# Forming a group's messages before the next group's placing one-hot on VectorE, in a graph attention layer

## The chip, the cores and the metric

The kernel runs on one core of one Trainium2 chip. The metric is the device time of one execution in microseconds. Three runs of the kernel before gave 1275.45, 1272.54 and 1271.82 us, so its time is the median, 1272.54 us. The hardware profiler recorded one further execution, and all rows shown below come from it.

## The reference

There are 6250 nodes with 96 features and 100000 edges, sorted by the node that they point to. The reference computes, with 8 heads of 12 numbers:

```
Q, K, V = x@Wq+bq, x@Wk+bk, x@Wv+bv          # per node
E       = edge_attr@We + be                  # per edge
score   = exp(clip(sum_12(K[src] * Q[dst] / sqrt(12) * E), -5, 5))   # per edge and head
msg     = V[src] * score
wV, Z   = segment_sum(msg, dst), segment_sum(score, dst)             # per node
out     = layernorm(x + wV / (Z + 1e-6))
```

## The kernel before, in words

A first part, some 125 us long, computes the tables of K and V (`kv_table`) and of Q (`q_table`) for all nodes and writes them to HBM. Then the edges are worked through in 99 groups: 96 groups of 8 tiles of 128 edges, and three shorter ones. This edge pass is what the change touches. Its program is fully unrolled, and the order on every engine is the order in which the code is written; nothing is scheduled. Each engine waits on counting semaphores: `sum_done`, for example, is raised by one when a group's scatter matmuls are done.

For a group g the work goes through the engines like this.

- GpSimd (POOL) gathers K and V rows of the group's source nodes, one indirect DMA for each tile, 8 to a group (L377). They go into `kv`, a ring of 8 groups. So the gathers of group g wait until the messages of group g-8 are formed (`msg_done`, L363), since that is the last reading of that part of the ring. From group 48 on (`CLOSE`) they also wait until the query matmuls of group g-2 are done (`q_done`, L365).
- TensorE (PE) projects the edge attributes (`psE`, L434), picks the destination's query by a matmul with a one-hot (`psQ`, L440), transposes the product `qe` to edge rows (`psT`, L451), and adds the messages to the nodes by matmuls with another one-hot, `place` (`psA`, L496). In its order stand, for group g: transposes of g+1, `psE` and `psQ` of g+2, then the scatter into `psA` of g. The function is `products`.
- ScalarE (ACT) copies `psE` to `qe` (L601), and takes the exponential of the clipped scores into the last 8 columns of `msg` (L615). Before that exponential it waits until the scatter of group g-2 is done, since `msg` has two buffers (L614).
- VectorE (DVE) does, in the function `arithmetic`: `qke` = transposed scores times K (L866), `qe` of the next group (L786), the sums over 12 (`logit`, L875), the clip (`clipped`, L881), the one-hot `place` of group g+1 (`make_place`, L774, which waits until the scatter of group g-1 is done, because `place` has two buffers), the messages `msg` of g (L890) and the one-hot `pick` of group g+3 (`make_pick`, L765).
- SyncE (SP) issues the other loads: the query windows `qwin`, two groups of edge attributes at a time (768 KB) and every fourth group a block of `rel_table` (1008 KB). They are issued as `q_done` rises.

Every four groups a block of nodes is finished. After the last scatter of a block, ACT copies `psA` out (L609), PE turns it (L461), and VectorE normalises it in twelve steps, `block_step` 0 to 11, strewn over the next groups. `between(n)` issues the step that stands for place n of the group by the table `BLOCK_PLACES`: in a block's first group, step 0 (`rzb`, L800) stands between `logit` and the clip, step 1 (L802) after the clip, step 2 (`yb`, L804) between `place` and `msg`, step 3 (L810) after `msg`. PE may begin the next block's scatter only when step 2 is done. In the third group, step 9 (L828) stands before `place`, step 10 (L831) between `place` and `msg`, and step 11 (`ob`, L838) after `msg`.

## Time and profile before

| | before |
|---|---|
| median of three runs | 1272.54 us |
| profiled execution: first to last instruction | 1265.2 us |
| what the runs have around that, against the median | 7.3 us |
| PE busy | 694.1 us (55%) |
| DVE busy | 620.3 us (49%) |
| ACT busy | 180.9 us (14%) |
| POOL busy | 758.5 us (60%) |
| granted TensorE clock, mean | 0.723 of full speed |

No engine is busy for more than 60% of the span. A busy share is an average over stages with different limits, so what the kernel is worth waiting for must be read from the waits. In the waits "remote" means that the profile found no instruction that ended just when the wait ended.

### The profile page before, as it was taken

Reading aid. Unit: us, or ns where it says so; the run is one execution under the profiler, and the core shown is the slowest. Engines: PE = TensorE matmul, PEld = TensorE weight load, DVE = VectorE, ACT = ScalarE, POOL = GpSimd, SP = SyncE. Lnnn points to the kernel's source line nnn. Section 1 sums busy time; section 2 is a strip of 40 time slices with the busy share of each in tenths; the row PEclk is TensorE's granted clock in tenths of the full one; section 3 lists DMA queues with packets and bytes.
Section 4 is the critical chain, followed back from the end, with each engine's and each line's share of the span. In section 5 each row is a group of like instructions: output and inputs, shape, how many; then the busy total and the mean of one; then the engine's idle time right before and its main releaser. Section 6 shows DMA issues by size and latency. Waiting matters only on the chain.

```text
span 1265.2 us, 11863 instructions
## 1 busy us (share of the span) xinstructions
PE 694.1 (55%) x3376; PEld 477.0 (38%) x3376; DVE 620.3 (49%) x1205; ACT 180.9 (14%) x343; POOL 758.5 (60%) x788
## 2 busy tenths in 40 slices
PE   4655646454445446436585575575545555565554
PEld 4554333243234324324353333343324333343332
DVE  1221435454355346436594554554545544544556
ACT  1224201111011011101120110110111110110111
POOL 7371456666656656656536566666666666666660
PEclk8657767768667767767796776677676786687777
DMA  7464254354355345444455445445435454454440
GB/s 185 156 198 139 79 149 128 102 158 130 105 142 139 106 127 150 115 125 127 135 144 146 125 114 157 127 115 156 126 105 164 129 140 133 127 135 135 121 115 28
DMA packets 89940, 165.51 MB, mean 131 GB/s; under 512 B 43315, under 2 KB 61908, under 8 KB 86840
## 3 DMA queue, kind: packets, MB, share of 16 engines
q1 hardware_dynamic: 52843, 89.34, 25.6%
q0 software_dynamic: 37024, 75.35, 21.4%
q8 instruction: 28, 0.46, 0.2%
q14 instruction: 45, 0.37, 0.1%
HBM read 152.22 MB, written 12.39 MB: 130 GB/s over the span
## 4 chain that ended last, share of the span: by engine, by line
another core or an unknown queue 40%; PE 21%; issue 17%; DVE 13%; ACT 6%; DMA 2%; SPq 0%; DVEq 0%
PE psE L434 7%; DVE qe L786 5%; ACT qe L601 5%; PE psA L496 4%; PE psT L451 4%; DVE logit L875 2%; DMA xt<-xT 1%; DVE msg L890 1%; PE psQ L416 1%; DVE qke L866 1%; PE psA L461 1%; PE psE L404 1%; DVE clipped L881 1%; DVE ob L838 1%
## 5 line engine op out<-in xcount | busy, mean ns | idle before, releaser
L377 POOL DMA_INDIRECT kv<-kv_table,idx x750 | 726.7, 969 | 468.7 <-issue 221.4
L496 PE MATMUL psA<-place,msg 128*104 128x104 f32 x1564 | 210.4, 301 | 289.9 <-DVE msg L890 220.6
L496 PEld LDWEIGHTS psA<-place,msg 128*104 128x104 f32 x1564 | 198.5, 213 | 318.6 <-DVE msg L890 235.0
L434 PE MATMUL psE<-ea,we 97*96 97x512 f32 x392 | 256.3, 790 | 0.0
L774 DVE TENSOR_TENSOR place<-psI,rel_tile 128x832 f32<-128x832 f32 (+1 forms) x99 | 98.5, 995 | 293.9 <-remote 293.9
L451 PE MATMUL psT<-identity,qe 96*128 96x96 f32 x782 | 114.7, 307 | 153.0 <-DVE qe L786 124.0
L601 ACT ACTIVATE qe<-psE 96x1024 f32<-96x1024 f32 (+1 forms) x99 | 99.9, 1009 | 622.0 <-remote 469.4
L786 DVE TENSOR_TENSOR qe<-psQ,qe 96x1024 f32<-96x1024 f32 (+1 forms) x99 | 119.1, 1203 | 82.3 <-ACT qe L601 33.8
L451 PEld LDWEIGHTS psT<-identity,qe 96*128 96x128 f32 x782 | 96.9, 181 | 165.1 <-DVE qe L786 128.3
L866 DVE TENSOR_TENSOR qke<-psT,kv 128x768 f32<-128x768 f32 (+1 forms) x99 | 92.9, 938 | 87.6 <-remote 86.9
L434 PEld LDWEIGHTS psE<-ea,we 97*96 97x96 f32 x392 | 75.8, 218 | 79.3 <-issue 79.3
L890 DVE TENSOR_TENSOR msg<-kv,msg 128x768 f32<-128x768 f32 (+1 forms) x99 | 93.0, 940 | 0.2
L875 DVE TENSOR_REDUCE logit<-qke 128x64 f32<-128x768 f32 (+1 forms) x99 | 91.5, 924 | 0.0
L440 PE MATMUL psQ<-q_parts,qwin 126*96 126x512 bf16 x196 | 69.7, 441 | 0.0
L615 ACT ACTIVATE msg<-clipped 128x64 f32<-128x64 f32 (+1 forms) x99 | 25.3, 256 | 259.2 <-DVE clipped L881 155.0
L440 PEld LDWEIGHTS psQ<-q_parts,qwin 126*96 126x96 bf16 x196 | 29.5, 150 | 79.9 <-issue 79.9
L765 DVE TENSOR_SCALAR q_parts<-q_parts,query_id 126x1024 bf16<-126x1024 bf16 x99 | 47.5, 481 | 12.2 <-DMA q_parts<-rel_table 12.2
L461 PE MATMUL psA<-identity,accT 104*128 104x104 f32 x73 | 17.3, 362 | 57.6 <-ACT accT L609 29.0
L800 DVE TENSOR_SCALAR rzb<-psA 128x24 f32<-128x24 f32 (+1 forms) x25 | 4.5, 181 | 68.2 <-PE psA L461 43.0
L375 POOL DMA_INDIRECT xg<-xrows,idx x32 | 31.3, 978 | 11.1 <-issue 9.5
L461 PEld LDWEIGHTS psA<-identity,accT 104*128 104x128 f32 x73 | 11.0, 208 | 62.6 <-ACT accT L609 32.8
L404 PE MATMUL psE<-wn,xt 97*128 97x192 f32 x52 | 16.3, 467 | 18.7 <-issue 14.6
(107 smaller groups left out, 356.8 us busy)
## 6 DMA issues: line engine op xcount, KB each, us to landing
ea<-eaT SPq DMA_DIRECT2D x49, 768.0 KB
q_parts<-rel_table SPq DMA_DIRECT2D x24, 1008.0 KB
kv<-kv_table,idx POOLq DMA_INDIRECT x750
qwin<-q_table SPq DMA_DIRECT2D x198, 23.6 KB
xb<-xrows SPq DMA_DIRECT2D x24, 144.0 KB
out<-ob SPq DMA_DIRECT2D x24, 144.0 KB
q_table<-q_parts SPq DMA_DIRECT2D x4, 720.0 KB
kv_table<-kv SPq DMA_DIRECT2D x2, 960.0 KB
```

Of the source, the lines that this page charges most:

```text
L377: pool.indirect_dma_start(kv[:, k, t], None, kv_table, sources).then_inc(kv_in[k], 16)
L434: last = nc.tensor.matmul(psE[0:D, h, 0:size], we[:], ea[:, k // 2 % 2, edge:edge + size], start=True, stop=True)
L440: last = nc.tensor.matmul(psQ[0:D, h, 0:size], qwin[0:QR, k % QRING, h], pick[0:QR, k % 2, h * GE // 2:h * GE // 2 + size], start=True, st ...
L451: last = nc.tensor.transpose(psT[:, t % 2, t // 2 * D:(t // 2 + 1) * D], qe[0:D, k % 2, t * P:(t + 1) * P], identity[0:D, 0:D])
L496: last = nc.tensor.matmul(psA[0:ML, off:off + PW], msg[:, s, t], place[:, s, t], start=opens, stop=closes)
L601: nc.scalar.activation(qe[0:D, k % 2, 0:edges], psE[0:D].rearrange("d b e -> d (b e)")[:, 0:edges], ACT.Copy).then_inc(e_up, 1)
L765: nc.vector.tensor_scalar(pick[0:QR, k % 2], rel[0:QR, k // BG % 2, k % BG * GE:(k % BG + 1) * GE], query_id[0:QR], None, ALU.is_equal).th ...
L774: nc.vector.tensor_tensor(place[:, k % 2, 0:nt], ps_ids[:, 0:PW].unsqueeze(1).broadcast_to([P, nt, PW]), rel_tile[:, bass.ds(g * T, nt)].u ...
L786: nc.vector.tensor_tensor(qe[0:D, k % 2, 0:edges], psQ[0:D].rearrange("d b e -> d (b e)")[:, 0:edges], qe[0:D, k % 2, 0:edges], ALU.mult). ...
L866: nc.vector.tensor_tensor(qke[:, 0:nt].rearrange("p (t b) d -> p b t d", **by_bank), psT[:, :, 0:nt // 2 * D].rearrange("p b (t d) -> p b ...
L875: nc.vector.tensor_reduce(logit[:, 0:nt * H], qke[:, 0:nt].rearrange("p t (h d) -> p (t h) d", h=H), AX.X, ALU.add).then_inc(logit_done, 1)
L890: nc.vector.tensor_tensor(msg[:, s, 0:nt, 0:D].rearrange("p t (h d) -> p t h d", h=H), kv[:, k, 0:nt, D:2 * D].rearrange("p t (h d) -> p t ...
```

## The change

On VectorE, `make_place` of the next group is moved from before the messages to behind them. The block steps of places 2 and 3 then stand directly behind each other, ahead of `msg`; the step of place 4 stands between `msg` and `place`. The wait of VectorE on `sum_done` ahead of `msg` is dropped; the wait on `wt_done`, which ScalarE raises only after its own wait on the same count of `sum_done`, stays. Nothing else is changed: the other engines have the same instructions in the same order.

```diff
                         nc.vector.tensor_scalar(clipped[:, s, 0:nt * H], logit[:, 0:nt * H], -5.0, 5.0, ALU.max,
                                                 ALU.min).then_inc(clip_done, 1)
                         between(2)
-                        if at + 1 < NG:
-                            make_place(r, k + 1, at + 1)
                         between(3)
-                        if at >= 2:
-                            dve.wait_ge(sum_done, g - 1)
                         dve.wait_ge(wt_done, g + 1)
                         nc.vector.tensor_tensor(
                             msg[:, s, 0:nt, 0:D].rearrange("p t (h d) -> p t h d", h=H),
                             kv[:, k, 0:nt, D:2 * D].rearrange("p t (h d) -> p t h d", h=H),
                             msg[:, s, 0:nt, D:ML].unsqueeze(3).broadcast_to([P, nt, H, HD]), ALU.mult).then_inc(msg_done, 1)
                         between(4)
+                        if at + 1 < NG:
+                            make_place(r, k + 1, at + 1)
                         if at + 3 < NG:
                             make_pick(r, k + 3, at + 3)
                         between(5)
```

VectorE in the first two groups of a block, before (`rzb`, `yb`, `bn`, `stat` belong to the block that has just ended; `q_parts` is the place in memory where `pick` lies):

```order
L881 TENSOR_SCALAR clipped<-logit 128x64 [waits logit_done,wt_done]
L802 RECIPROCAL rzb<-rzb 128x24 [waits block_steps]
L774 TENSOR_TENSOR place<-psI,rel_tile 128x832 [waits sum_done]
L804 TENSOR_TENSOR yb<-psA,rzb 128x288 [waits block_steps]
L890 TENSOR_TENSOR msg<-kv,msg 128x8x96 [waits wt_done,sum_done]
L810 TENSOR_TENSOR yb<-yb,xb 128x288 [waits xb_in1,block_steps]
L765 TENSOR_SCALAR q_parts<-q_parts,query_id 126x1024 [waits q_done,rel_in0]
L813 BN_STATS bn<-yb 128x6 [waits block_steps]
L813 BN_STATS bn<-yb 128x6 x2
L866 TENSOR_TENSOR qke<-psT,kv 128x2x4x96 [waits kv_in1,t_done]
```

The same place after the change (the message line is L886 there):

```order
L881 TENSOR_SCALAR clipped<-logit 128x64 [waits logit_done,wt_done]
L802 RECIPROCAL rzb<-rzb 128x24 [waits block_steps]
L804 TENSOR_TENSOR yb<-psA,rzb 128x288 [waits block_steps]
L886 TENSOR_TENSOR msg<-kv,msg 128x8x96 [waits wt_done]
L810 TENSOR_TENSOR yb<-yb,xb 128x288 [waits xb_in1,block_steps]
L774 TENSOR_TENSOR place<-psI,rel_tile 128x832 [waits sum_done]
L765 TENSOR_SCALAR q_parts<-q_parts,query_id 126x1024 [waits q_done,rel_in0]
L813 BN_STATS bn<-yb 128x6 [waits block_steps]
L813 BN_STATS bn<-yb 128x6 x2
L866 TENSOR_TENSOR qke<-psT,kv 128x2x4x96 [waits kv_in1,t_done]
```

`place` has moved two places back, behind the messages and step 3, and takes its wait on `sum_done` with it.

VectorE in the third group of a block, before:

```order
L881 TENSOR_SCALAR clipped<-logit 128x64 [waits logit_done,wt_done]
L828 TENSOR_SCALAR spread<-spread 128x3 [waits block_steps]
L774 TENSOR_TENSOR place<-psI,rel_tile 128x832 [waits sum_done]
L831 TENSOR_TENSOR spread<-spread 128x3 [waits block_steps]
L890 TENSOR_TENSOR msg<-kv,msg 128x8x96 [waits wt_done,sum_done]
L838 TENSOR_SCALAR ob<-yb,stat,spread 128x96 [waits block_steps,ob_out]
L838 TENSOR_SCALAR ob<-yb,stat,spread 128x96 x2
L765 TENSOR_SCALAR q_parts<-q_parts,query_id 126x1024 [waits q_done,rel_in1]
```

And after the change:

```order
L881 TENSOR_SCALAR clipped<-logit 128x64 [waits logit_done,wt_done]
L828 TENSOR_SCALAR spread<-spread 128x3 [waits block_steps]
L831 TENSOR_TENSOR spread<-spread 128x3 [waits block_steps]
L886 TENSOR_TENSOR msg<-kv,msg 128x8x96 [waits wt_done]
L838 TENSOR_SCALAR ob<-yb,stat,spread 128x96 [waits block_steps,ob_out]
L838 TENSOR_SCALAR ob<-yb,stat,spread 128x96 x2
L774 TENSOR_TENSOR place<-psI,rel_tile 128x832 [waits sum_done]
L765 TENSOR_SCALAR q_parts<-q_parts,query_id 126x1024 [waits q_done,rel_in1]
```

Here the three instructions that write the finished rows come between the messages and `place` too.

## Rows read from the trace of the kernel before

**Rows 1.** The page, part 4: shares of the chain that ended last.

```profile
another core or an unknown queue 40%; PE 21%; issue 17%; DVE 13%; ACT 6%; DMA 2%; SPq 0%; DVEq 0%
```

**Rows 2.** Waits from 165.3 to 594.5 us: who waited for what, us, times, longest.

```profile
DVE place L774 <- remote: 181.1, 16, 13.1
POOL kv L377 <- issue: 80.1, 263, 0.3
POOL kv L377 <- DVE msg L890: 79.2, 17, 5.9
DVE rzb L800 <- PE psA L461: 23.8, 9, 12.4
```

**Rows 3.** Timeline, 600 to 624 us: start, us, engine, line [idle before, its end].

```profile
600.91 0.94 DVE L866 TENSOR_TENSOR qke<-psT,kv 128x768 f32<-128x768 f32 x1
...
603.76 1.88 PE L434 MATMUL psE<-ea,we 97*96 97x512 f32 x4
603.95 0.19 DVE L881 TENSOR_SCALAR clipped<-logit 128x64 f32<-128x64 f32 x1
604.18 0.26 ACT L615 ACTIVATE msg<-clipped 128x64 f32<-128x64 f32 x1 [2.90 <-issue]
...
613.49 0.95 POOL L377 DMA_INDIRECT kv<-kv_table,idx  x1 [0.31 <-issue]
617.25 1.02 DVE L774 TENSOR_TENSOR place<-psI,rel_tile 128x832 f32<-128x832 f32 x1 [13.10 <-remote]
617.40 1.02 ACT L601 ACTIVATE qe<-psE 96x1024 f32<-96x1024 f32 x1 [12.96 <-remote]
618.19 0.95 DVE L890 TENSOR_TENSOR msg<-kv,msg 128x768 f32<-128x768 f32 x1
619.05 0.48 DVE L765 TENSOR_SCALAR q_parts<-q_parts,query_id 126x1024 bf16<-126x1024 bf16 x1
619.19 3.10 PE L496 MATMUL psA<-place,msg 128*104 128x104 f32 x16 [13.12 <-DVE msg L890]
619.41 0.95 POOL L377 DMA_INDIRECT kv<-kv_table,idx  x1 [4.97 <-DVE msg L890]
619.45 0.95 DVE L866 TENSOR_TENSOR qke<-psT,kv 128x768 f32<-128x768 f32 x1
620.32 1.21 DVE L786 TENSOR_TENSOR qe<-psQ,qe 96x1024 f32<-96x1024 f32 x1
```

**Rows 4.** Windows: us, busy of PE, PEld, DVE, ACT, POOL (instructions), clock, DMA, GB/s.

```profile
604.70:617.20 12.50, 1.37 (x5) 0.33 (x3) 0.00 (x0) 0.00 (x0) 7.56 (x8) 0.75 0.32 89
625.00:651.00 26.00, 22.90 (x132) 13.81 (x132) 24.80 (x49) 6.09 (x12) 3.79 (x4) 0.94 0.48 132
```

**Rows 5.** Groups of instructions on POOL, 165.3 to 594.5 us: busy, mean ns, idle.

```profile
L377 POOL DMA_INDIRECT kv<-kv_table,idx x280 | 271.8, 971 | 159.3 <-issue 80.1 <-DVE msg L890 79.2
```

**Rows 6.** The same on POOL, 675.5 to 1195.5 us.

```profile
L377 POOL DMA_INDIRECT kv<-kv_table,idx x352 | 339.8, 965 | 179.4 <-issue 108.0 <-remote 70.5 <-PE psQ L440 0.9
```

**Rows 7.** Timeline, 699 to 724 us: a cycle behind group 48.

```profile
699.71 0.95 POOL L377 DMA_INDIRECT kv<-kv_table,idx  x1 [3.33 <-remote]
...
706.78 1.63 PE L496 MATMUL psA<-place,msg 128*104 128x104 f32 x16
...
716.64 1.02 DVE L774 TENSOR_TENSOR place<-psI,rel_tile 128x832 f32<-128x832 f32 x1 [6.61 <-remote]
...
722.32 0.96 DVE L866 TENSOR_TENSOR qke<-psT,kv 128x768 f32<-128x768 f32 x1 [2.60 <-remote]
722.38 1.02 ACT L601 ACTIVATE qe<-psE 96x1024 f32<-96x1024 f32 x1 [12.13 <-remote]
723.44 0.94 POOL L377 DMA_INDIRECT kv<-kv_table,idx  x1 [4.02 <-issue]
```

**Rows 8.** Timeline, 599 us: a gather beside the messages.

```profile
598.93 0.95 DVE L890 TENSOR_TENSOR msg<-kv,msg 128x768 f32<-128x768 f32 x1
...
599.60 1.10 POOL L377 DMA_INDIRECT kv<-kv_table,idx  x1 [0.30 <-issue]
```

## The prediction, as it was made before the changed kernel was run

> **What bounds the kernel now.** I read the page first and found no busy engine; the largest share of the chain that ended last, 40%, is idle time that ends with a semaphore whose giver the profile can't name [rows 1]. So I read the waits of a steady stretch next. From 165.3 to 594.5 us VectorE stands 181.1 us before `place`, in 16 waits of up to 13.1 us, all "remote", and POOL stands 79.2 us before a gather until VectorE has formed messages, in 17 waits [rows 2]. `place` waits for one thing alone, the scatter of the group before the last. The timeline shows what is odd about it. PE ends `psE` at 603.76 + 1.88 = 605.6 us; ACT, which waits for just that, begins at 617.40, after 12.96 us of idling, and VectorE's `place` at 617.25 after 13.10 us [rows 3]. In that time PE, DVE and ACT do next to nothing while POOL issues its 8 gathers [rows 4]. What PE has finished is seen by the others only after POOL has stopped: the last gather ends at 613.49 + 0.95 = 614.4, the wait ends 2.8 us later. I call this a hold. A second place shows its beginning: the gathers start at 699.71, the scatter ends at 706.78 + 1.63 = 708.4, 8.7 us into them, and `place`, which waits for it, starts at 716.64 [rows 7]. What VectorE and ACT give to each other is not held: at 603.95 and 604.18 the exponential follows the clip at once, while PE's results are already late [rows 3].
>
> So the pass up to group 48 goes in cycles. POOL gathers as long as messages have been formed 8 groups back, PE's results come through in roughly the first 7 to 9 us, then all stand until POOL itself runs out of messages and stops. Between 165.3 and 594.5 us there are 280 gathers, 35 groups; 429.2 / 35 = 12.26 us for a group. Of that POOL's own pace is (271.8 + 80.1) / 280 = 1.257 us for a gather, 10.05 us for a group, and the 79.2 us of waits make 2.26 [rows 5, 2]. A typical cycle is 16 gathers and a pause of 4.97 us: 2.8 us until the hold ends, and then 617.25 to 619.41, 2.2 us, in which VectorE does `place` and `msg` [rows 3]. Without gathers the same work runs free: 5 messages in 26.0 us with VectorE busy for 24.8 of them [rows 4], some 6 us a group.
>
> **The change part by part.** It removes no instruction and adds none; a wait on `sum_done` goes that ACT has already made, worth 0.
>
> *Messages during the hold.* In the cycle shown, the exponential ends at 604.18 + 0.26 = 604.4. With `place` no longer ahead, the messages are formed at about 604.5 to 605.4, instead of 618.19 to 619.14. POOL needs them at 614.4, so this pause of 4.97 us goes. That is the gain one sees first. But what is late next is the following group's messages, and for these VectorE needs `psT` from PE, which is held until POOL stops. So the pause isn't removed, it comes one group later.
>
> *The pause in the steady state.* When the hold ends, VectorE now stands before `place` with the messages already spent. Ahead of the next `msg` are then `place` 0.94 (start to start, 617.25 to 618.19), `pick` 0.40 (619.05 to 619.45), `qke` 0.87 (to 620.32), `qe` 1.21, `logit` about 0.9, the clip 0.3, the exponential 0.3, and `msg` 0.95 with 0.3 to POOL's start [rows 3]: 6.1 us instead of 2.2. If instead the query or edge result of the next group was caught by the hold, VectorE stands before `qe`: 1.2 for ACT's copy, then 1.2 + 0.9 + 0.3 + 0.3 + 0.95 + 0.3 = 5.1. Where it is a block's first group, VectorE stands before `rzb`, which needs the last scatter copied and turned; after that only clip, exponential, step 2 and `msg` are left, about 3.8. The mean is 5.0, and the whole pause 2.8 + 5.0 = 7.8 us in place of 5.0.
>
> *How many groups fit a cycle.* The clock of the hold starts with POOL. With the messages of two groups formed by some 13 us after the hold's end, the third needs PE's `psE` and `psQ` of a further group; going through the durations of [rows 3] I find these finished about 8 to 9 us after POOL has started again, just where the hold sets in (8.7 us was too late in [rows 7]). So I take two groups in most cycles and three in one of four. With two, a cycle is 2 x 10.05 + 7.8 = 27.9 us, 13.95 a group, 1.7 more than now. With three, (30.15 + 7.8) / 3 = 12.65, 0.4 more. A block's first group can't be formed in a hold at all, since `rzb` waits on the last scatter; that cuts cycles of three short. A quarter of the cycles with three gives about 1.35 a group, for 35 groups +47 us. At the end of the stretch POOL must wait anyhow until PE has caught up, and one pause less is in the way: -5.
>
> *Behind group 48.* There POOL waits for `q_done` and not for messages: 70.5 us remote and 0.9 us by name on 44 groups [rows 6]. At a hold's end VectorE stands before `qke` [rows 7], and after the change it will stand there as well; `qe`, PE and the next gather follow it as before. Here I take 0. Bounds: the message comes 0.94 earlier where `place` isn't held (below nothing: -0.9 for each of 25 cycles, -22), or a `pick` that is made later costs a query result, one extra pause of 4.0 in a few cycles, +20.
>
> *The gap that `place` filled.* Between clip and `msg` lies the exponential, 0.3 us with its semaphores; `place` stood there. Now VectorE idles for it where no block step stands at place 2. That costs only where VectorE sets the pace, the 26 us of [rows 4] and a little more: 7 groups by 0.3, +2. If it were on the path everywhere it would be 99 x 0.3 = 30.
>
> *Gathers beside messages.* The gather that starts at 599.60 beside `msg` takes 1.10 us, the others 0.95 [rows 8, 3]. That is 0.15 by 35, at most +5, and mostly the same pairs meet already; I take 0. The Trainium skill (GPSIMD Engine Reference, Specifications) says that VectorE instructions with two SBUF inputs contend with GpSimd for its SBUF interface, which speaks against forming messages during gathers; by a full lock of 0.95 us for each message it would be +33, by the row at most +5, and the row decides.
>
> The sum against the profiled execution: 1265.2 + 47 - 5 + 0 + 2 = 1309; with the 7.3 us by which the median stands above its span, 1317 us, 3.5% slower.
>
> **The rivals.**
>
> *Nearly all cycles hold three groups.* For it: the results of PE are only about a microsecond late. Against it: the block's first group. 35 x 0.4 - 5 + 2 = +11, 1284 us. If on the contrary all hold two, it is 35 x 1.7 - 3 = +56, 1329 us.
>
> *Faster: the hold opens while POOL runs on.* In [rows 7] `place` got its semaphore at 716.64, in the midst of the gathers and not after them; there loads of SP were in flight. If with messages formed ahead POOL runs on over such openings, the pause stays 5 us but comes once in three groups or more: (30.15 + 5.0) / 3 = 11.7, 0.55 less than now, 35 x 0.55 = 19 us; with no pauses at all it would be all 79 us of [rows 2]. I take -32 for it, 1240 us. It decides from the point at which a cycle holds four groups at my pause, or three with the old one. Against it: in the stretch of [rows 2] 16 waits make 181 us, so most last to POOL's stop.
>
> *No effect.* POOL's pauses only shift and the sum of a cycle stays: one group more before each pause, a longer pause behind it. That is between the two above, 1272 us.
>
> **How the numbers follow.** Mostly two groups a cycle (the forecast, and all two): 0.50. Nearly all three: 0.17. No effect: 0.11. Faster: 0.18. Something worse behind group 48 on top: 0.04. A difference of 0.3%, 4 us, is what a measurement of this kernel can tell from none. That gives slower 0.70, same 0.12, faster 0.18. The range goes from 1248, which takes in most of the faster case, to 1342, the all-two case with 13 us of the bound behind group 48. The forecast's own range is 1295 to 1335.
>
> **What would show it.** Right: up to group 48 POOL's waits for messages are fewer than 17 but their sum grows from 79 to about 125 us; VectorE's waits before `place` shrink while those before `qe` (for ACT's copy or the query result), `rzb` and `qke` grow; messages lie in the midst of gathers where nothing else moves; POOL's pace stays at 1.26 us. Behind group 48 the cycle stays at 23 to 24 us for 16 gathers. Wrong: runs of 24 or 32 gathers with pauses of 5 us, then it is faster; or 16 gathers with the pauses of now. If VectorE's busy time or POOL's mean of 971 ns changes by more than 3%, something is at work that I haven't seen.

## The result, and the profile after

| | before | changed |
|---|---|---|
| median of 4 runs each, same chip | 1273.99 us (1271.82 to 1277.34) | 1317.16 us (1304.74 to 1323.02) |
| ratio | | 1.031, 95% interval 1.026 to 1.036 |
| span of the profiled execution | 1265.2 us | 1321.3 us (its own time 1323.02) |

The changed kernel is 3.1% slower, 1317.16 us where 1317 was forecast. That is better than the forecast deserves: one of its terms was 15 us too large and two were 5 and 10 us too small. And on another chip, on which nothing of what is called a hold occurs, the same change made the kernel 1.5% faster. Both are shown below.

The page of the changed kernel, its span, busy times and the chain that ended last:

```profile
span 1321.3 us, 11766 instructions
PE 701.4 (53%) x3376; PEld 470.2 (36%) x3376; DVE 638.9 (48%) x1205; ACT 180.4 (14%) x343; POOL 758.5 (57%) x788
another core or an unknown queue 41%; PE 21%; issue 18%; DVE 13%; ACT 5%; DMA 1%; SPq 0%; DVEq 0%
```

The shares of the chain are those of before within a point [rows 1], and POOL is busy for exactly as long, 758.5 us. So the loss isn't work. It is in the waits. First POOL's, in the stretch of the changed kernel that answers to [rows 2] (188.3 to 620.6 us, 33 groups in 13 unbroken runs of gathers), then the group of its gathers, which answers to [rows 5]:

```profile
POOL kv L377 <- DVE msg L886: 102.3, 13, 10.1
```

```profile
L377 POOL DMA_INDIRECT kv<-kv_table,idx x264 | 255.2, 967 | 179.6 <-DVE msg L886 102.3 <-issue 77.3
```

A wait for messages is now 102.3 / 13 = 7.9 us long, against 79.2 / 17 = 4.7 before [rows 2], and there are 13 of them for 33 groups instead of 17 for 35. A gather's own pace is (255.2 + 77.3) / 264 = 1.259 us, as before.

What VectorE waits for in the same stretch, changed kernel:

```profile
DVE qke L866 <- remote: 57.7, 15, 6.8
DVE qe L786 <- remote: 43.3, 8, 8.2
DVE place L774 <- remote: 41.6, 8, 13.8
DVE place L774 <- PE psA L496: 32.4, 3, 15.8
DVE qe L786 <- ACT qe L601: 23.4, 14, 7.2
DVE rzb L800 <- PE psA L461: 9.3, 6, 5.3
```

And the kernel before, from 165.3 to 594.5 us, beside the rows for `place` and `rzb` in [rows 2]:

```profile
DVE qe L786 <- remote: 3.8, 2, 1.9
DVE qe L786 <- ACT qe L601: 3.4, 4, 1.1
DVE qke L866 <- remote: 1.0, 2, 0.6
```

The waits before `place` fall from 181.1 us to 41.6 + 32.4 = 74.0, those before `qe` and `qke` rise from some 8 us to 124. VectorE now meets the hold at whatever it does next with something from PE.

One whole cycle of the changed kernel, three groups long, from its timeline (start, us, engine, line [idle before, what ended it]). POOL has been gathering since 399.61:

```profile
405.47 1.88 PE L434 MATMUL psE<-ea,we 97*96 97x512 f32 x4
...
407.19 0.60 PE L440 MATMUL psQ<-q_parts,qwin 126*96 126x512 bf16 x2
...
412.38 0.96 DVE L866 TENSOR_TENSOR qke<-psT,kv 128x768 f32<-128x768 f32 x1 [3.06 <-remote]
414.52 1.02 ACT L601 ACTIVATE qe<-psE 96x1024 f32<-96x1024 f32 x1 [8.66 <-remote]
416.65 1.22 DVE L786 TENSOR_TENSOR qe<-psQ,qe 96x1024 f32<-96x1024 f32 x1 [3.31 <-remote]
...
419.55 0.96 DVE L886 TENSOR_TENSOR msg<-kv,msg 128x768 f32<-128x768 f32 x1 [0.32 <-ACT msg L615]
420.78 0.94 POOL L377 DMA_INDIRECT kv<-kv_table,idx  x1 [1.11 <-issue]
...
425.06 0.33 PE L496 MATMUL psA<-place,msg 128*104 128x104 f32 x1 [0.98 <-issue]
...
429.53 0.95 POOL L377 DMA_INDIRECT kv<-kv_table,idx  x1 [0.30 <-issue]
...
433.54 1.02 DVE L774 TENSOR_TENSOR place<-psI,rel_tile 128x832 f32<-128x832 f32 x1 [13.03 <-remote]
433.69 1.02 ACT L601 ACTIVATE qe<-psE 96x1024 f32<-96x1024 f32 x1 [14.18 <-remote]
434.88 0.95 DVE L866 TENSOR_TENSOR qke<-psT,kv 128x768 f32<-128x768 f32 x1
435.74 1.21 DVE L786 TENSOR_TENSOR qe<-psQ,qe 96x1024 f32<-96x1024 f32 x1
...
438.51 0.96 DVE L886 TENSOR_TENSOR msg<-kv,msg 128x768 f32<-128x768 f32 x1
439.74 0.94 POOL L377 DMA_INDIRECT kv<-kv_table,idx  x1 [9.26 <-DVE msg L886]
```

Read it from the end. The last gather ends at 429.53 + 0.95 = 430.48, the hold 3.0 us later (`place` and ACT's copy start together, 433.54 and 433.69). Then VectorE goes through `place`, `pick`, `qke`, `qe`, `logit`, the clip and `msg` before POOL may go on at 439.74: 6.2 us, and 9.26 in all, where the kernel before had 2.8 + 2.2 [rows 3]. The upper lines show why three groups fit: PE's results do reach the others in the midst of the gathers, one by one, 7 to 9 us late. `psE` ends at 405.47 + 1.88 = 407.35 and ScalarE copies it at 414.52; `psQ` ends at 407.79 and `qe` starts at 416.65. And the third group's messages at 419.55 come just in time (POOL stands for 1.11 us instead of 0.30). Between 423 and 433 us PE itself does nine of the sixteen scatter matmuls of a group in pieces, one every 0.7 to 2.1 us; the last seven follow in a row from 433.46, as the hold ends.

Behind group 48, the gathers that answer to [rows 6] (719.1 to 1249.3 us), and POOL's waits there:

```profile
POOL kv L377 <- remote: 59.8, 18, 4.1
POOL kv L377 <- PE psQ L440: 21.4, 6, 10.2
```

The 352 gathers take 530.2 us instead of 520.0. The wait for query results by name grew from 0.9 to 21.4 us. Nearly all of that are two pauses, 10.18 us before the gather at 890.63 and 9.98 us before that at 1037.2, each behind 24 gathers in a row. The first of them:

```profile
883.83 0.49 ACT L609 ACTIVATE accT<-psA 104x384 f32<-104x384 f32 x1 [15.90 <-remote]
...
886.24 3.20 PE L434 MATMUL psE<-ea,we 97*96 97x512 f32 x4
...
888.30 0.48 DVE L765 TENSOR_SCALAR q_parts<-q_parts,query_id 126x1024 bf16<-126x1024 bf16 x1
...
889.27 0.60 PE L440 MATMUL psQ<-q_parts,qwin 126*96 126x512 bf16 x2
...
890.63 0.94 POOL L377 DMA_INDIRECT kv<-kv_table,idx  x1 [10.18 <-PE psQ L440]
```

Here the hold caught the last scatter of a block: ScalarE could copy `psA` only at 883.83, after 15.90 us of idling. `psQ` begins as `psE`, which stands ahead of it on PE, comes to its end (886.24 + 3.20 = 889.44); `pick` was ready before that, at 888.78. The second pause has the same form.

Where the spans differ, 1321.3 - 1265.2 = 56.1 us: the time to the first gather of the edge pass proper 148.5 - 140.6 = 7.9, in the first part, which the change doesn't touch and where one load landed later (VectorE waited 30.7 us for it, before 14.8); from there to the first gather of group 48, 549.2 - 511.4 = 37.8; behind it 623.6 - 613.2 = 10.4. The profiled execution is also the slowest of its four, which lie between 1304.74 and 1323.02 us, so a term of 5 or 10 us, read from one execution of each kernel, is of the size of what executions differ by.

### The profile page after: what moved, and what is told of

Its sections match the earlier page's. It is cut to its first block, busy times and chain, and to the rows that moved or that the text cites. A ratio compares the mean times of both kernels' runs of the same rounds, so it can differ in the third digit from the quotient of the medians.

```text
span 1321.3 us, 11766 instructions
## 1 busy us (share of the span) xinstructions
PE 701.4 (53%) x3376; PEld 470.2 (36%) x3376; DVE 638.9 (48%) x1205; ACT 180.4 (14%) x343; POOL 758.5 (57%) x788
## 3 DMA queue, kind: packets, MB, share of 16 engines
q1 hardware_dynamic: 52843, 89.34, 24.3%
## 4 chain that ended last, share of the span: by engine, by line
another core or an unknown queue 41%; PE 21%; issue 18%; DVE 13%; ACT 5%; DMA 1%; SPq 0%; DVEq 0%
PE psE L434 8%; DVE qe L786 5%; PE psT L451 4%; ACT qe L601 4%; DVE logit L875 2%; PE psA L496 2%; DVE qke L866 1%; PE psQ L416 1%; DMA xt<-ones 1%; DVE msg L886 1%; DVE q_parts L765 1%; DVE place L774 1%; PE psE L404 1%; DVE clipped L881 1%
## 5 line engine op out<-in xcount | busy, mean ns | idle before, releaser
L434 PE MATMUL psE<-ea,we 97*96 97x512 f32 x392 | 274.6, 840 | 0.0
L451 PE MATMUL psT<-identity,qe 96*128 96x96 f32 x782 | 120.1, 317 | 278.0 <-DVE qe L786 195.5
L496 PE MATMUL psA<-place,msg 128*104 128x104 f32 x1564 | 195.7, 271 | 93.8 <-issue 92.3
L496 PEld LDWEIGHTS psA<-place,msg 128*104 128x104 f32 x1564 | 182.0, 186 | 116.8 <-issue 105.0
L434 PEld LDWEIGHTS psE<-ea,we 97*96 97x96 f32 x392 | 79.8, 229 | 84.9 <-issue 84.9
L886 DVE TENSOR_TENSOR msg<-kv,msg 128x768 f32<-128x768 f32 (+1 forms) x99 | 93.6, 946 | 17.5 <-ACT msg L615 10.9
L461 PEld LDWEIGHTS psA<-identity,accT 104*128 104x128 f32 x73 | 10.9, 208 | 178.6 <-ACT accT L609 159.9
L440 PE MATMUL psQ<-q_parts,qwin 126*96 126x512 bf16 x196 | 72.8, 459 | 0.0
```

Source lines behind the costliest of these rows:

```text
L434: last = nc.tensor.matmul(psE[0:D, h, 0:size], we[:], ea[:, k // 2 % 2, edge:edge + size], start=True, stop=True)
L440: last = nc.tensor.matmul(psQ[0:D, h, 0:size], qwin[0:QR, k % QRING, h], pick[0:QR, k % 2, h * GE // 2:h * GE // 2 + size], start=True, st ...
L451: last = nc.tensor.transpose(psT[:, t % 2, t // 2 * D:(t // 2 + 1) * D], qe[0:D, k % 2, t * P:(t + 1) * P], identity[0:D, 0:D])
L496: last = nc.tensor.matmul(psA[0:ML, off:off + PW], msg[:, s, t], place[:, s, t], start=opens, stop=closes)
L886: nc.vector.tensor_tensor(msg[:, s, 0:nt, 0:D].rearrange("p t (h d) -> p t h d", h=H), kv[:, k, 0:nt, D:2 * D].rearrange("p t (h d) -> p t ...
```

## The experiments

Twelve runs were made, in four sets on three chips. Each ratio is to the kernel before on the same chip. The first two chips, with three of the sets, don't hold back PE's results, the last one does.

### First set: where messages are waited for, and what holds

**The kernel before, closing from group 8.** POOL waits for the query results from group 8 on, not from 48.

```diff
-CLOSE = 48
+CLOSE = 8
```

> The kernel before, with one constant changed: POOL's wait for the query matmuls of the group before the last holds for all groups from 8 on, not from 48 on. My theory (after a hold ends, the time until POOL may restart is what counts; with this wait it restarts 1 us later, whatever VectorE has in front of the messages): the whole pass goes in the cycles now seen behind group 48, 23.6 us for two groups; POOL's eighth group starts at some 155 us, then 91 groups by 11.8 make 1229, with the tail some 1245 us of span and a median of 1250 (1240 to 1265). Rival (POOL's lead of 8 groups is what keeps the pass fed): slower than before, 1290 or more.

Measured: 1080.01 us, ratio 1.024 (1.021 to 1.028).

**The changed kernel, closing from group 8.** The same edit in the changed order.

> The changed kernel with the same constant changed. POOL no longer waits for messages, so if the loss of 43 us comes from messages that POOL waits for after a hold, it is gone: within 12 us of the kernel before with the same constant, some 1255. Rival (the order itself costs, by the gap before the messages, by the later place and pick, or by the block steps, anywhere in the pass): the 43 us stay, some 1290.

Measured: 1062.91 us, ratio 1.008 (1.005 to 1.010).

**The changed order with the scatter waited for.** `place` stays behind the messages, but the messages wait for the last scatter.

```diff
+                        if at >= 1:
+                            dve.wait_ge(sum_done, g)
                         dve.wait_ge(wt_done, g + 1)
                         nc.vector.tensor_tensor(
                             msg[:, s, 0:nt, 0:D]...
```

> The changed kernel, with a wait put in ahead of the messages on the very count of scatters that place of the next group waits for. The order is that of the change, but no messages are formed in a hold any more; when it ends they are the first thing VectorE does, and POOL restarts 0.94 us earlier than in the kernel before. My theory: pauses of 4.0 us in place of 5.0, 17 of them: 1257 (1245 to 1272), so 60 us faster than the changed kernel. Rival (the order costs): 1300 to 1320, and a second one (messages early are good, something else is bad): slower than the changed kernel.

Measured: 1040.3 us, ratio 0.986 (0.982 to 0.990).

**The changed kernel without most of its loads.** Edge attributes and relation blocks are loaded once and used again for all later groups; the loads behind the first ones are left out, and the groups behind compute with old data.

```diff
-                        if at % 2 == 1 and at + 3 < NG:
+                        if not first and at % 2 == 1 and at + 3 < NG:
-                        if j == BG - 1 and at + BG + 1 < NG:
+                        if not first and j == BG - 1 and at + BG + 1 < NG:
```

> The changed kernel without the loads of edge attributes and of the relative table after the first two of each (left out: the groups behind compute with old data). They are 98% of what the hardware queue moves in the pass, but POOL's gathers stay. If holds open in the midst of gathers because these loads break the stream of the gathers' packets, there are no openings now: all cycles have two groups at 13.95, and behind group 48 nothing changes: 1330 (1310 to 1345). If the loads' traffic is what holds back PE's semaphores, the holds go: below 1200.

Measured: 1029.87 us, ratio 0.978 (0.974 to 0.982). The hardware queue moved 28.49 MB in place of 89.34; of what it moves in the edge pass the loads left out are some 84% by the sizes of the issues, and not the 98% of the expectation.

All four expectations were written for a chip on which the kernel before takes 1273 us. Here it took 1054.49 us, and none of the four kernels shows a hold: POOL gathers without pause. So this set says nothing on how a cycle is built, nor on whether loads make the holds. What it says is the sign: the changed order, which had lost 3%, is ahead by more than 1% (1062.91 against 1080.01 us with the wait from group 8, 1040.3 against 1054.49 with the wait for the scatter). Closing from group 8 costs both orders about as much, 26 us in before's order and 22 in the changed one (against its time in the second set, on another chip).

### Second set: the same change on a chip without holds

**The kernel before, and the changed kernel, both as they are**, with a profile of each.

> The kernel before, unchanged, for a second profile of it beside the changed kernel on one chip. On a chip like that of the first comparison: 1272 us, with POOL in runs of 16 gathers and VectorE waiting some 290 us before place. On a chip like that of the first four experiments: 1054 us, POOL in one run of 718 gathers at 991 ns, no semaphore of PE late.

> The changed kernel, unchanged. If this chip holds PE's semaphores back: 3% slower than before, by longer pauses of POOL. If it does not, there are no pauses that could grow, and POOL's gathers set the time: with CLOSE at 8 the changed order had them at 967 ns and the old one at 991, 24 ns by 750 = 18 us, and the times differed by 17. So here some 15 us faster than before, 1039 (1030 to 1048) against 1054. Rival (that difference came of the constant, not of the order): the same as before, 1054, or slower by the gap before the messages.

Measured: before 1055.71 us; changed 1040.86 us, ratio 0.985 (0.982 to 0.987), as expected for a chip without holds.

The kernel before on this chip: POOL's waits, then from the page POOL's gathers and VectorE's `qke` (busy, mean ns, idle before):

```profile
POOL kv L377 <- issue: 226.5, 743, 0.3
L377 POOL DMA_INDIRECT kv<-kv_table,idx x750 | 742.7, 990 | 248.9 <-issue 226.5
L866 DVE TENSOR_TENSOR qke<-psT,kv 128x768 f32<-128x768 f32 (+1 forms) x99 | 93.4, 943 | 341.9 <-DMA kv<-kv_table,idx 340.6
```

The changed kernel on the same chip:

```profile
L377 POOL DMA_INDIRECT kv<-kv_table,idx x750 | 728.2, 971 | 251.2 <-issue 226.7
L866 DVE TENSOR_TENSOR qke<-psT,kv 128x768 f32<-128x768 f32 (+1 forms) x99 | 93.5, 944 | 291.5 <-DMA kv<-kv_table,idx 290.2
```

No wait on this chip is "remote". (The chain that ended last says nothing here: it could be followed over only some 2% of the span.) POOL never stops for longer than 0.3 us in the edge pass, and VectorE stands before `qke` until gathered rows have landed: the gathers set the time. One by one they are shorter in the changed order, 971 ns instead of 990. The 718 gathers of the pass last from 105.7 to 1035.8 us in the kernel before, 930.1 us, and from 107.4 to 1023.1 us in the changed one, 915.7 us. These 14.4 us are nearly the whole gain of 14.85. Why a gather should be shorter was then the question.

**The changed order with the scatter waited for, once more.**

> The changed order with a wait that keeps messages out of a hold, again. On a chip with holds my theory says 1257 (1245 to 1272), faster than before and 60 us faster than the changed kernel; the rival, that the order itself costs, 1300 to 1320. On a chip without holds there is nothing for the wait to do: the same as the changed kernel within 5 us.

Measured: 1039.98 us, ratio 0.984 (0.981 to 0.987), gathers 975 ns. That is the time of the changed kernel; VectorE hasn't to wait there.

**The kernel before without gathers**: those of groups 8 and later are left out, and the old rows in the ring are used in their place.

```diff
+                        if first and at >= U:
+                            return
```

> The kernel before without POOL's gathers from group 8 on (left out: later groups use the old rows of K and V). If the gathers make the holds, none is left on any chip: no wait before place over 1 us, 6.2 us a group, 125 + 99 x 6.2 = 740 us (700 to 790). If the holds come from the loads or from PE itself, a chip that has them stays above 900.

Measured: 702.04 us, ratio 0.665. Its page:

```profile
PE 553.2 (79%) x3376; PEld 379.8 (54%) x3376; DVE 606.9 (87%) x1205; ACT 181.4 (26%) x343; POOL 62.5 (9%) x70
```

The time lies in the range of the expectation. The other engines alone need 702 us, so without holds some 350 us of the kernel are there for the gathers. Since POOL never pauses on this chip, what moves on VectorE can matter in the pass only by the length of the gathers. Whether the gathers make the holds this run can't say, as the chip has none.

### Third set: what lengthens a gather

**Pick first.** The order of before, with the picking one-hot in front of `place` instead of behind the messages.

```diff
                         between(2)
+                        if at + 3 < NG:
+                            make_pick(r, k + 3, at + 3)
                         if at + 1 < NG:
                             make_place(r, k + 1, at + 1)
                         ...
                         between(4)
-                        if at + 3 < NG:
-                            make_pick(r, k + 3, at + 3)
```

> The order of before, with one move: the picking one-hot of three groups ahead is formed in front of the placing one-hot instead of behind the messages, so that messages and picking one-hot no longer stand back to back. Theory A (on a chip where the gathers follow one another without pauses, they set the time, and the gather that lies across two long VectorE instructions one directly behind the other is the slow one, 1.25 us beside 0.95): the mean gather goes from 990 ns to about 971 ns as in the changed kernel, and the time to about 1041 us against 1055, ratio 0.986. Rival B (what helped the changed kernel is that the messages stand ahead of the place, so that they are done earlier): the gathers stay at 990 ns and the time at 1055 us. On a chip where TensorE's finished results are held back during gathers: theory A says the hold decides, and as place still stands ahead of the messages the time is within 1% of before's there.

Measured: 1061.73 us, ratio 1.003 (1.000 to 1.005). Its gathers:

```profile
L377 POOL DMA_INDIRECT kv<-kv_table,idx x750 | 748.9, 999 | 252.2 <-issue 226.1 <-DVE msg L892 20.9 <-DMA kv_table<-kv 4.6
```

Both the theory, 971 ns and 1041 us, and the rival, 990 and 1055, miss: the gathers are the longest of all, 999 ns, and the time is 0.3% above that of before, an interval that barely leaves out none. So "two long instructions back to back" was wrong. What is right shows in any of the traces once the slow gathers are laid beside the messages. The kernel before, without holds:

```profile
506.17 0.95 DVE L890 TENSOR_TENSOR msg<-kv,msg 128x768 f32<-128x768 f32 x1
506.69 1.25 POOL L377 DMA_INDIRECT kv<-kv_table,idx  x1 [0.30 <-issue]
```

The changed kernel, without holds, at two places:

```profile
501.05 0.96 DVE L886 TENSOR_TENSOR msg<-kv,msg 128x768 f32<-128x768 f32 x1 [0.32 <-ACT msg L615]
...
501.97 0.95 POOL L377 DMA_INDIRECT kv<-kv_table,idx  x1 [0.30 <-issue]
...
522.18 0.96 DVE L886 TENSOR_TENSOR msg<-kv,msg 128x768 f32<-128x768 f32 x1 [0.32 <-ACT msg L615]
522.41 1.55 POOL L377 DMA_INDIRECT kv<-kv_table,idx  x1 [0.30 <-issue]
```

The first gather ends at 507.94, 0.82 us behind the end of `msg` at 507.12. The one at 522.41 ends at 523.96, 0.82 us behind 523.14. The gather at 501.97 begins as `msg` ends and takes its 0.95. And the gather of [rows 8], 599.60 + 1.10 = 600.70, ends 0.82 us behind its `msg`, at 599.88. So a gather that begins while the messages are being formed stands still until they are done, and then needs 0.82 us. I went through all 750 gathers of each kernel for this (worked out from the starts and ends in the traces; "caught" is a gather that begins at least 0.1 us after a `msg` did and before its end; the excess is over 0.945 us, what a gather takes beside an idle VectorE):

| kernel, no holds | caught | their mean | excess of these | of all 750 |
|---|---|---|---|---|
| before | 69 | 1.304 us | 24.8 us | 34.0 us |
| changed | 55 | 1.202 us | 14.1 us | 19.4 us |
| pick first | 71 | 1.347 us | 28.5 us | 40.2 us |

Counted from the very start of `msg` it is 77, 56 and 75 gathers, with an excess of 29.5, 14.1 and 31.5 us; 73 of the 77 and 42 of the 56 are lengthened at all (the expectations of the fourth set speak of 76 and 41). The others begin in the last 0.14 us of `msg`, where ending 0.82 us behind it is no delay, or, three of them, within 12 ns of its start. The median end of a caught gather is 0.82 us behind the end of `msg` in all three. In the same traces a gather that begins inside `qke` or `place`, which are as long, takes 0.945 to 0.968 us on the mean. And it is only the gather that waits: the messages that begin while a gather is under way, 75 in the kernel before, take 0.95 us as they do elsewhere, and so does their gather. The order only sets at which phase of POOL's 1.25 us the messages begin: in all three kernels VectorE starts from rows that a gather has just brought, so a `place` or a `pick` more or less ahead of `msg` shifts it against the gathers.

A page of the Trainium skill speaks against my taking this cost at nothing: by SBUF — State Buffer, section "SBUF: two separate sides", a VectorE instruction with two SBUF inputs and a GpSimd instruction that reads SBUF exclude each other, and the one that starts second waits until the other is done. The traces agree with it for a gather that starts second, and not for a message that does. `msg` reads `kv` and the weights, both in SBUF; `qke`, `qe` and `place` read one operand from PSUM.

**The changed order with the scatter waited for, on this chip too.**

> The changed order with one wait added: the messages of a group may only begin when TensorE has summed the group before (as they would have in before's order, behind the place). On a chip without holds: as in the earlier two runs, about 0.985 of before. On a chip with holds: theory A (the messages that are made during the hold, and POOL's restart behind place plus messages, cost the 3%) has the messages back behind the hold, but place now stands behind them: about 1.00 to 1.03; rival B (the wait in front of the messages loses the third group of a cycle): over 1.03.

Measured: 1042.02 us, ratio 0.987 (0.984 to 0.990), gathers 975 ns. No holds again, so it doesn't tell the two theories on the hold apart.

### Fourth set: weights in PSUM, on a chip with holds

ScalarE takes the exponential a second time, into a free part of the bank of `psI`, and `msg` reads the weights from there. In before's order `place`, which reads the same bank, is made to wait until that is written.

```diff
+                            nc.scalar.activation(weights_up(k % 2, nt), clipped[...], ACT.Exp).then_inc(wt_done, 1)
...
                         between(2)
+                        dve.wait_ge(wt_done, 2 * (g + 1))        # in before's order only
...
-                            msg[:, s, 0:nt, D:ML].unsqueeze(3).broadcast_to([P, nt, H, HD]), ALU.mult)
+                            weights_up(s, nt).unsqueeze(3).broadcast_to([P, nt, H, HD]), ALU.mult)
```

**Before's order:**

> The order of before, but ScalarE writes the weights a second time, into PSUM, and the messages' multiplication takes them from there: it then reads one operand from SBUF (kv) and one from PSUM, instead of both from SBUF. The place, which reads the same PSUM bank, waits until the weights are written (up to 0.5 us on VectorE, which idles 3.4 us a group for kv on a chip without holds). Theory C (a gather whose start falls into a running message multiplication waits for its end and then takes 0.82 us more; 76 of 96 messages caught a gather so in the kernel before, 30 us in all, and 41 in the changed one, 14 us; the order only moves how often that happens): on a chip without holds the gathers shorten from 990 to about 950 to 958 ns, and the time from 1056 to about 1028, ratio 0.97 to 0.98, whatever the order. Rival D (any long busy stretch of VectorE lengthens a gather, the operands' place does not matter): 990 ns and 1055 us here, and the changed order 971 ns and 1040 us. On a chip with holds: theory says gathers shorten alike, and the holds still set the groups per cycle: 0.99 to 1.00.

Measured: 1360.09 us, ratio 1.036 (1.031 to 1.041); the kernel before took 1310.44 us on this chip.

**The changed order:**

> The changed order, with the weights written a second time into PSUM and taken from there by the messages' multiplication. Theory C: gathers of about 950 to 958 ns instead of 971, and about 1028 us on a chip without holds, within 3 us of the same edit in before's order, so that the order no longer makes a difference there. Rival D: 971 ns and 1040 us. On a chip with holds: as the changed kernel there, about 1.03 of before, less 0.01 for the shorter gathers.

Measured: 1363.94 us, ratio 1.040 (1.036 to 1.044).

POOL's gathers in the two (before's order, then the changed one):

```profile
L380 POOL DMA_INDIRECT kv<-kv_table,idx x750 | 712.4, 950 | 570.4 <-issue 222.5 <-DVE msg L897 211.5 <-remote 63.8
```

```profile
L380 POOL DMA_INDIRECT kv<-kv_table,idx x750 | 710.6, 947 | 583.9 <-issue 223.5 <-DVE msg L892 164.3 <-PE psQ L443 124.1
```

A pair from the changed order with weights in PSUM, a gather that begins 0.1 us into `msg`:

```profile
415.85 0.95 DVE L892 TENSOR_TENSOR msg<-kv,psI 128x768 f32<-128x768 f32 x1 [0.44 <-ACT psI L621]
415.96 0.94 POOL L380 DMA_INDIRECT kv<-kv_table,idx  x1 [0.30 <-issue]
```

The part of theory C on the gathers is shown: 35 gathers of the one kernel and 49 of the other begin while `msg` runs, and their mean is 0.953 and 0.946 us. With one operand in PSUM a message costs a gather nothing, in either order; the rival (any busy VectorE) is out. What that gives in time where gathers set it, the 1028 us of the expectation, no run shows, since this chip has holds.

The times are where I was wrong. I expected 0.99 to 1.00 and about 1.02. The gathers are the shortest of all, and yet the kernels are the slowest. POOL's and VectorE's waits of before's order with the weights in PSUM, from 190 to 630 us:

```profile
POOL kv L380 <- DVE msg L897: 113.9, 17, 7.9
DVE rzb L806 <- PE psA L464: 108.2, 9, 13.9
```

A pause is 113.9 / 17 = 6.7 us there, against 4.7 in [rows 2], though the cycles are two groups long as before. The hold now also catches the block's last scatter (`rzb` waits 108.2 us in 9 times; in [rows 2] 23.8 in 9). Its restart, from the timeline of the same kernel:

```profile
403.07 0.95 POOL L380 DMA_INDIRECT kv<-kv_table,idx  x1 [0.30 <-issue]
407.16 0.49 ACT L612 ACTIVATE accT<-psA 104x384 f32<-104x384 f32 x1 [13.22 <-remote]
...
409.25 1.02 DVE L780 TENSOR_TENSOR place<-psI,rel_tile 128x832 f32<-128x832 f32 x1 [0.20 <-ACT psI L621]
...
410.56 0.94 DVE L897 TENSOR_TENSOR msg<-kv,psI 128x768 f32<-128x768 f32 x1
411.77 0.95 POOL L380 DMA_INDIRECT kv<-kv_table,idx  x1 [7.75 <-DVE msg L897]
```

The hold ends 3.1 us after the last gather; copy, turn, `rzb`, clip, exponentials, `place`, step 2 and `msg` take 4.6 more. Every second pause is of this kind, 7.7 to 7.9 us, the others are about 5.5 us. So before's order, with none of the changed order's early messages, loses as much here, and in its long pauses it is a block's last scatter that the hold caught. Why a wait of up to 0.4 us before `place` moves the hold onto the block's end I can't say: that the cycle of two groups locks to the block of four, in one phase or the other, would do it, but no run shows that. Nor was the kernel before profiled on this chip, where it takes 36 us more than in the first comparison, and the changed kernel didn't run there as it is. The edit also puts a second exponential before `msg`, so its 1.036 and 1.040 are not the cost of the order alone.

## Why the prediction was right, and where it wasn't

*What bounds the kernel: holds.* Right for the chip on which it was timed. The experiments add that the hold isn't part of every chip: the same kernel takes 1055 us where it is absent, and of the waits that end "remote", 181.1 us before `place` in [rows 2] alone, none is left.

*Messages during the hold; the pause comes one group later.* Right. 13 pauses of 7.9 us on the mean (4.7 to 10.1) stand where the forecast had 7.8, and its longest path, 6.1 us for `place` to `msg`, measured 6.2 in the cycle shown.

*Groups per cycle.* Mis-sized. I took three groups in one cycle of four, which by the forecast's own cycles is (0.75 x 27.9 + 0.25 x 37.95) / 2.25 = 13.5 us a group, +1.26 and 44 us, not +1.35 and 47. Of the 13 runs of gathers, 7 hold three groups and 6 hold two. That gives (7 x 3 x 10.05 + 6 x 2 x 10.05 + 13 x 7.9) / 33 = 13.16 us a group, +0.9 on 12.26, over 35 groups about +32 where the forecast had +47. (Straight from the stretch, (620.6 - 188.3) / 33 = 13.10.) The step that failed is "finished about 8 to 9 us after POOL has started again, just where the hold sets in": PE's results go on reaching the others in the midst of the gathers, 7 to 9 us late. This is half of the "faster" rival's mechanism, "the hold opens while POOL runs on"; it brought the third group, and not the fourth that the rival needed.

*The end of the stretch, -5 us.* It wasn't seen: from the first gather of the pass proper to group 48 it is +37.8 for 40 groups, 0.94 each, with nothing given back: the pause before group 48 is 27.3 us long, in the kernel before 22.3. The 47 - 5 = 42 of the forecast stand against this 37.8.

*Behind group 48, 0.* Mis-sized: +10.4 us, inside the bound of +20, but not by the mechanism named there, a `pick` that is made later. Most cycles do stay at some 23.5 us for 16 gathers. What is new are the two pauses of 10.2 and 10.0 us, where the kernel before has none over 4.0: POOL ran three groups in a row, and the hold then caught the block's last scatter. `pick` was ready before `psE` let `psQ` begin. "A block's first group can't be formed in a hold at all", which the forecast used up to group 48, was left out here.

*The gap that `place` filled, +2.* VectorE waits 17.5 us for the exponential in the whole run, 10.9 of it by name, at places where it mostly isn't the bound. No run isolates its share.

*Gathers beside messages, 0.* Right for the comparison made, wrong as a reason. With holds the excess over 0.945 us is 17.9 us before and 18.7 changed, and it doesn't set the time. Without holds it is 34.0 against 19.4, and it is the whole effect. That this is the whole effect is worked out from traces; the run that would remove it on such a chip, the weights in PSUM, wasn't made there. "By the row at most +5" went by one gather of 1.10 us that was caught late; one caught early takes 1.55. And "some pairs meet already" should have been asked the other way round: whether fewer would meet.

*The sum.* 37.8 + 10.4 = 48.2 measured between the spans for what was forecast as 44, less 5.6 for what lies around the span (1.7 us in this execution, where I carried over 7.3), plus 7.9 of the first part that the change has nothing to do with. The medians, which leave the one execution's accidents out, differ by 43.2. So the 1317 us is hit by terms that cancel, one too large and two too small: that the sum came out to the microsecond is luck.

*The rivals.* All threes, 1284, and no effect, 1272, are out on the chip of the comparison. "Faster" was right elsewhere, for a reason that none of my rivals named.

*Its own tests.* "Fewer than 17 but their sum grows": 13, and 102.3 us instead of the 125 forecast. VectorE's waits before `place` shrink and those before `qe` and `qke` grow: yes, but those before `rzb` fell, from 23.8 to 9.3 us. "Messages in the midst of gathers": yes, 419.55. POOL's pace 1.26: yes. POOL's mean of 971 ns is 967 in the changed kernel's stretch (969 and 970 over the whole runs), and so the sentence that would have warned of the port stayed silent; even on the chip without holds it changed by 2%, less than the 3% set there. VectorE's busy time went from 620.3 to 638.9 us, 3.0%, just at that bound. Added up one by one its instructions take 702.8 and 705.3 us, so they overlap less and are hardly longer.

What stays open: what a hold is, why some chips have it, whether gathers or loads are needed for it (both runs on that fell on chips without holds), and whether the changed order with a wait, which was meant to put the messages back behind the hold, would lose there. All three of its runs fell on chips without holds. The ends of PE's matmuls are modelled in the profile, so the rows don't tell late results from late signals, and whether the lower granted clock goes before the holds or comes of them isn't shown either. The changed kernel itself ran on one chip with holds and on one without. No kernel that computes everything beat the faster of the two orders by more than can be told (1039.98 against 1040.86 us at best); which of them is better depends on the chip.

## What to carry to other kernels

When a producer stops and starts in cycles, count what stands between the restart's first signal and the producer's own release, in the order of the instructions: work moved behind the release comes back in front of the next one, and the pause grows by it. A VectorE instruction like `msg`, with both operands in SBUF, holds up a gather that starts inside it, so look at such pairs gather by gather, not at the mean. With one operand in PSUM it doesn't; whether that pays in time where gathers set it would have to be measured. Time a small change on more than one chip before its sign is believed: here it was +3.1% on one and -1.5% on another.

## What the runs showed of the hardware

- The same kernel takes 1274 us in the first comparison, then 1054, 1056 and 1310 us on three chips. On the two near 1055 us nothing of PE's is seen late; with holds ACT and VectorE stand up to 13 to 19 us for results that PE's records show as done. The mean granted clock goes along, 0.71 in the changed kernel with holds and 0.78 without.
- In a hold PE's own instructions can be drawn out, as in the cycle shown of the changed kernel: sixteen scatter matmuls from 423.5 to 435.0 us in place of 1.6 us in a row.
- A gather instruction takes 0.945 us and 0.30 to the next. If `msg` is running when it begins, it ends 0.82 us after `msg` does, so up to 1.78 us long; with the weights in PSUM it takes 0.95 us. A `msg` that begins inside a gather takes its 0.95 us, and so does the gather. Leaving out most of the loads shortened the mean gather to 957 ns, since fewer were caught (28 instead of 55).
